# Graph layer with resnorm: the edge products of a group in one burst every second turn, its sum behind the next burst, attention earlier

## Chip, core and metric

One core of a Trainium2 chip runs the whole program. The time is device microseconds of one execution; the kernel before took 1297.51 us (median of three runs, 1295.53 to 1299.25). Five engines work from queues of their own, each in its own order, and meet at semaphores only: TensorE (PE; PEld is its weight loading), VectorE (DVE), ScalarE (ACT), GpSimd (POOL) and SyncE (SP, which issues DMAs).

## What is computed

There are 8192 nodes with 256 values each and 131072 edges, sorted by destination, with 64 values each. All of it is float32.

```python
msg = relu(x[src] + edge_attr @ w_e + b_e)
agg = segment_sum(msg, dst)
h_local = bn1(relu((x + agg) @ w1 + b1) @ w2 + b2 + x)
h_attn = bn2(attention(x in blocks of 32 nodes, 4 heads) @ out_w + out_b + x)
out = h_local + h_attn
out = bn3(out + relu(out @ m_w1 + m_b1) @ m_w2 + m_b2)
result = layernorm(x + out)
```

## The kernel before

**Edges.** They are worked through in 128 groups of 1024, each of four pairs (a pair q is two tiles of 128 edges, 128x512 numbers), in 256 turns of two pairs; eight more turns end the program. For a pair, POOL gathers the rows of x by two indirect DMAs into one of seven buffers `xg` (L430); before every second pair it waits until the pair six earlier has been read (L427). For 14 of the 512 pairs SP and ACT fetch the rows instead, one DMA a row (L329, L463). DVE adds b_e to the rows and puts the sum into one of four PSUM banks (`seed`, L681: "additions of b_e"); the bank must have been read by the message four pairs earlier. PE adds the edge product on top (`products(d)`, L867: eight matmuls for the two pairs of turn d). ACT makes the message by relu into SBUF (`message`, L469). 

**Sums.** PE sums a group's four messages with a one-hot matrix (`sum_group`, L882, 16 matmuls, "S"), ACT copies the sum (`copy_agg`, L474, "C"), PE transposes the copy (`transpose_agg`, L891, two transposes, "X"), and DVE adds it to `aggT` at the places of the group's destinations (`add_agg`, L714, four additions, "A"). S of the next group waits for A of this one, since both use bank G. In the kernel before, S of group n ends turn 2n+1 on PE, C ends the same turn on ACT, and X comes in turn 2n+2 behind the products of that turn.

**Attention** goes over 16 slabs J of 512 nodes. Its steps have fixed turns, counted from `heads_base(J)`: q, k (each in two halves, ACT adds the bias as it copies: L482, L490), scores (PE, L938), maximum and subtraction on DVE (L726, L731), exponential on ACT (L496), normalising and transposing on DVE (L738 to L747), v, and the product with v ("av"), both copied by ACT. **Node blocks** b (12 of 512 nodes, 6 of 256, 4 of 128) have plans of the same kind, `NODES`, `NODES_256` with `FIRST_256`, and `NODES_128`: w1 (PE; ACT makes h1, L515), B (PE adds attention's output product and w2's; DVE makes `o`, L758; ACT makes z, L523), m1 (ACT makes h2, L529), m2 (DVE adds, L767), T (PE transposes; DVE adds x and takes the statistics, L779 to L787), log and y (ACT, DVE), out. All PE products of attention and blocks have line 837, that of the helper `product`.

**Order.** Each engine has a loop over turns, and in a turn a fixed order. PE: products, X, attention, node steps, S. ACT: messages, copies of attention, of node steps, C, then its row DMAs. DVE: additions of b_e for the next turn, A, one-hot matrix, attention, node steps. An engine that comes to a wait stands until it is met, and all that is behind it in its queue stands too. SP issues the loads and stores in the order of turns.

Of the kernel before, what the change touches and what calls it, by code (L numbers as in the profile page):

```python
# [15 lines left out]
CC = C // 128  # L16
P = 128
TG = 8
GE = TG * P
NG = E // GE  # L20
PG = TG // 2
NP = NG * PG
# [37 lines left out]
def heads_base(J):  # L60
    return max(16 * J - 12, 12 * J)

# [7 lines left out]
             "y": (7,), "xn": (2,), "out": (8,)}  # L70
FIRST_256 = {12: 211, 13: 217, 14: 223, 15: 229, 16: 235, 17: 243}
NODES_128 = {
# [8 lines left out]
}  # L81
LASTB = 21


SUMS = {2 * n + 1: n for n in range(NG)}
TURNS = 264
# [27 lines left out]
def before(b, stage):  # L114
    return sum(uses(n, stage) for n in range(b))
# [9 lines left out]
def nodes_in(turn, stages):  # L125
    found = []
    for b in range(len(BLOCKS)):
        if b < 12:
            plan, base = NODES, 16 * b + 19
        elif b < 18:  # L130
            plan, base = NODES_256, FIRST_256[b]
        else:
            plan, base = NODES_128[b], 0
        found += [(b, s, n) for s in stages for n, at in enumerate(plan[s]) if base + at == turn]
    return found
# [89 lines left out]
def program(nc, k):  # L225
# [3 lines left out]
    with ExitStack() as ctx:  # L229
# [47 lines left out]
        def cols(b):  # L277

            w = BLOCKS[b][1]
            at = 0 if w == FULL else b % 2 * 256  # L280
            return slice(at, at + w)
# [36 lines left out]
        def _(sp):  # L318
# [44 lines left out]
            for turn in range(TURNS):  # L363
# [5 lines left out]
                if turn in (2, 12):  # L369
                    load_xT(1 if turn == 2 else 2)  # L370
                if turn % 16 == 13 and NXT <= (turn + 19) // 16 < NJ:
                    load_xT((turn + 19) // 16)
                for J, _, pair in heads_in(turn - 1, ("av",)):
# [66 lines left out]
        def _(act):  # L440
# [101 lines left out]
            for turn in range(TURNS):  # L542
                for q in (2 * turn, 2 * turn + 1):
                    if q < NP:
                        message(q)
                for J, stage, n in heads_in(turn, ("q", "k", "soft", "v", "av")):
                    attention(J, stage, n)
                for b, stage, use in nodes_in(turn, ("z", "w1", "m1", "log")):
                    node(b, stage, use)
                if turn in SUMS:  # L550
                    copy_agg(SUMS[turn])
                for row in range(ACT_ROWS * ROWS):
                    if act_turn(row) == turn:
                        fetch_row(SP_ROWS + row // ROWS, row % ROWS)
# [5 lines left out]
        def _(dve):  # L560
# [245 lines left out]

            seed(0)
            seed(1)
            make_onehot(0)
            for turn in range(TURNS):  # L810
                for q in (2 * turn + 2, 2 * turn + 3):
                    if q < NP:
                        seed(q)
# [20 lines left out]
        def _(pe):  # L834
# [135 lines left out]
            def node(b, stage, use):  # L970
                n0, w = BLOCKS[b]
                at, to = cols(b), bank(b, stage)
                J, of_slab = part(b)
                if stage == "w1":
# [13 lines left out]
                    for c, of in chunks(b, "w1", use):  # L988
                        ins = product(to[:, of], CC, lambda a: k.w1[:, a, c * P:(c + 1) * P],
                                      lambda a: aggT[:, a, n0:n0 + w])  # L990
                    ins.then_inc(s_p1, 1)
                if stage == "B":
                    early = b == LASTB
                    if use:
                        pe.wait_ge(s_o, before(b, "B") + use)
                    else:
                        pe.wait_ge(s_oc, (n0 + w + NB - 1) // NB)
                    if early:
                        for c, of in chunks(b, "B", use):
                            product(to[:, of], CC, lambda a: k.owT[:, a, c * P:(c + 1) * P],  # L1000
                                    lambda a: k.oT[:, J % NOT, a, of_slab], start=c == 0,
                                    stop=False, skip=True)
                    if not use:
                        pe.wait_ge(s_h1, before(b + 1, "w1"))
# [36 lines left out]

            for turn in range(TURNS):
                if turn < ND:
                    products(turn)
                if turn - 1 in SUMS:
                    transpose_agg(SUMS[turn - 1])
                weights(turn)
                for J, stage, n in heads_in(turn, ("q", "k", "sc", "v", "av")):
                    attention(J, stage, n)
                for b, stage, use in nodes_in(turn, ("T", "m2", "m1", "B", "w1")):  # L1050
                    node(b, stage, use)
                if turn in SUMS:
                    sum_group(SUMS[turn])
            with pe.If(pe.value_load(k.bad_i[0:1, 0:1], min_val=0, max_val=1) > 0):
                pe.wait_ge(s_go, 1)
                general_tensor(nc, k, g, pe)
# [309 lines left out]
```

## Time and profile before

| | |
|---|---|
| median of three runs | 1297.51 us |
| the profiled execution, time of its own | 1296.03 us |
| its span, from first to last instruction | 1294.2 us |
| PE busy | 1154.5 us (89%) |
| POOL busy | 944.9 us (73%) |
| DVE, ACT busy | 826.7 us (64%), 541.2 us (42%) |
| granted TensorE clock, mean | 0.969 |

Busy time of an engine is the union of its instructions. The time around them is either a wait for something that the profile names, or "issue": the engine waited for nothing that the profile shows. POOL's 73% are the instructions that write the gathers' descriptors; between two of them there is a fixed stretch of "issue". ACT's row DMAs count as issue too, not as busy.

### The profile page before, as it was taken

To read this page: it belongs to the slowest core of one execution; us is meant where nothing else is said; L and a number is where in the kernel's file an instruction comes from. 1 tells how busy PE (TensorE), PEld (TensorE's weight loads), DVE (VectorE), ACT (ScalarE), POOL (GpSimd) and SP (SyncE) were. 2 spreads that over 40 slices of the span, in tenths; PEclk is the share of its full clock that TensorE was granted. 3 is DMA by queue.
4 is the path that set the end of the run, shared out by engine and by line. 5 is a ranking of instruction groups with operands and counts; after the bars stand their busy time and mean duration, and the time that the engine had idled before them with its cause. 6 is when DMAs were issued, how large, how long until landed. Compare 5 with 4: busy or idle time off the path is not lost.

```text
span 1294.2 us, 28246 instructions
## 1 busy us (share of the span) xinstructions
PE 1154.5 (89%) x7309; PEld 647.4 (50%) x7309; DVE 826.7 (64%) x2090; ACT 541.2 (42%) x1077; POOL 944.9 (73%) x1004
## 2 busy tenths in 40 slices
PE   6787989998899899998989999998989998998896
PEld 3444454544445444444544545454444555765675
DVE  5847486767566576755758666575756667557563
ACT  1343434444344435434344443443434443443353
POOL 7777777777777777777777777777777777675770
PEclk7898999999999999999999999999999998999999
DMA  8554555655555555565555555555655565554550
GB/s 316 154 170 141 175 156 175 174 173 180 170 165 169 164 182 172 160 183 148 183 173 175 165 165 176 166 175 174 172 164 154 183 183 147 168 160 126 175 155 26
DMA packets 119282, 216.50 MB, mean 167 GB/s; under 512 B 24784, under 2 KB 69584, under 8 KB 119120
## 3 DMA queue, kind: packets, MB, share of 16 engines
q0 software_dynamic: 47808, 130.61, 35.0%
q1 hardware_dynamic: 67312, 79.47, 19.6%
q10 hardware_dynamic: 4000, 4.61, 1.0%
q8 instruction: 59, 0.97, 0.3%
q14 instruction: 103, 0.84, 0.2%
HBM read 197.82 MB, written 16.78 MB: 166 GB/s over the span
## 4 chain that ended last, share of the span: by engine, by line
PE 58%; DVE 11%; ACTq 8%; ACT 7%; issue 7%; POOL 6%; DMA 2%; DVEq 0%; SPq 0%
PE bank L837 33%; PE bank L867 12%; PE bank L882 7%; POOL xg L430 6%; ACTq L463 6%; ACT msg L469 4%; DVE bank L681 3%; PE bank L891 3%; ACTq L311 2%; DVE dif L731 2%; DVE mx L726 2%; PE bank L938 1%; DMA xT<-in_xT_dram 1%; DVE aggT L714 1%; ACT kbd L490 1%
## 5 line engine op out<-in xcount | busy, mean ns | idle before, releaser
L430 POOL DMA_INDIRECT xg<-in_x_dram,srcs x996 | 944.0, 948 | 317.4 <-issue 290.0
L469 ACT ACTIVATE msg<-bank 128x512 f32<-128x512 f32 x512 | 277.8, 595 | 543.6 <-PE bank L867 286.7
L681 DVE TENSOR_TENSOR bank<-xg,bank 128x512 f32<-128x512 f32 x498 | 327.4, 690 | 138.1 <-DMA xg<-in_x_dram,srcs 93.0
L867 PE MATMUL bank<-we,ea 64*128 64x256 f32 x2048 | 301.7, 415 | 35.5 <-DVE bank L681 35.5
L867 PEld LDWEIGHTS bank<-we,ea 64*128 64x128 f32 x2048 | 183.1, 192 | 179.7 <-issue 124.1
L714 DVE TENSOR_TENSOR aggT<-bank,aggT 128x64 f32 x512 | 115.2, 225 | 169.1 <-PE bank L891 115.2
L882 PE MATMUL bank<-msg,onehot 128*32 128x256 f32 x2048 | 141.1, 394 | 49.0 <-ACT msg L469 48.4
L837 PE MATMUL bank<-xT,iwT 128*128 128x512 f32 x256 | 128.2, 624 | 7.6 <-DMA xT<-in_xT_dram 4.0
L837 PE MATMUL bank<-o,m 128*128 128x512 f32 (+2 forms) x352 | 125.6, 491 | 4.6 <-DVE o L758 4.4
L882 PEld LDWEIGHTS bank<-msg,onehot 128*32 128x32 f32 x2048 | 54.4, 111 | 141.6 <-ACT msg L469 96.9
L837 PE MATMUL bank<-h,m 128*128 128x512 f32 (+2 forms) x352 | 116.6, 479 | 2.1 <-ACT h L529 2.1
L837 PEld LDWEIGHTS bank<-o,m 128*128 128x128 f32 x352 | 60.7, 193 | 41.3 <-issue 27.9
L837 PEld LDWEIGHTS bank<-h,m 128*128 128x128 f32 x352 | 60.0, 190 | 41.3 <-issue 34.9
L837 PE MATMUL bank<-aggT,w 128*128 128x512 f32 (+2 forms) x176 | 66.1, 510 | 15.7 <-DVE xn L779 13.8
L474 ACT COPY agg<-bank 128x256 f32<-128x256 f32 x128 | 47.5, 371 | 70.8 <-PE bank L882 67.2
L837 PEld LDWEIGHTS bank<-xT,iwT 128*128 128x128 f32 x256 | 45.4, 198 | 51.9 <-issue 46.0
L767 DVE TENSOR_TENSOR z<-bank,z 128x512 f32<-128x512 f32 (+2 forms) x44 | 23.1, 543 | 72.1 <-PE bank L837 71.9
L891 PE MATMUL bank<-ident,agg 128*128 128x128 f32 x256 | 57.7, 308 | 7.5 <-ACT agg L474 7.5
L837 PE MATMUL bank<-iwT,xT 128*128 128x256 f32 x256 | 64.3, 395 | 0.0
L837 PE MATMUL bank<-oT,owT 128*128 128x512 f32 (+2 forms) x176 | 63.6, 485 | 0.0
L529 ACT ACTIVATE h<-bank,mb 128x512 f32<-128x512 f32 (+2 forms) x88 | 47.5, 570 | 37.3 <-PE bank L837 36.9
L837 PE MATMUL bank<-h,w 128*128 128x512 f32 (+2 forms) x176 | 62.1, 476 | 0.0
(92 smaller groups left out, 938.9 us busy)
## 6 DMA issues: line engine op xcount, KB each, us to landing
rows<-in_x_dram SPq DMA_DIRECT2D x2304, 1.0 KB
ea<-in_ea_dram SPq DMA_DIRECT2D x128, 256.0 KB
rows<-in_x_dram ACTq DMA_DIRECT2D x1280, 1.0 KB
xg<-in_x_dram,srcs POOLq DMA_INDIRECT x996
xT<-in_xT_dram SPq DMA_DIRECT2D x32, 256.0 KB, 4.2
aggT<-in_xT_dram SPq DMA_DIRECT2D x32, 256.0 KB, 4.0
oT_dram<-oT SPq DMA_DIRECT2D x32, 256.0 KB
xn<-in_x_dram SPq DMA_DIRECT2D x32, 256.0 KB
```

The costliest lines, as they stand in the source:

```text
L311: _, of = nc.values_load_multi_w_load_instructions(k.of_rows[at:at + 1, col:col + LOADED], engines=(engine,), min_val=0, max_val=(N - 1) * ...
L430: pool.indirect_dma_start(xg[:, slot % NX, n * C:(n + 1) * C], None, t["x"], bass.IndirectOffsetOnAxis(k.srcs[:, at:at + 1], 0)).then_inc( ...
L463: act.dma_start(row_bytes[e:e + 1, row_buffer(n), two * 4 * C:(two + 1) * 4 * C], x_bytes[0:1, bass.ds(of_row[0][i % LOADED], 4 * C)]).the ...
L469: nc.scalar.activation(msg[:, q % NM, :], EA[q % 4][:, :], ACT.Relu).then_inc(s_msg, 1)
L474: nc.scalar.copy(k.agg[:, :], G[:, 0:C]).then_inc(s_agg, 1)
L529: ins = nc.scalar.activation(k.h2[:, c, at], bank(b, "m1")[:, of], ACT.Relu, bias=k.mb1[:, c:c + 1])
L681: nc.vector.tensor_tensor(EA[q % 4][:, :].rearrange("p (a c) -> p a c", a=2), pair.rearrange("p (a c) -> p a c", a=2), KB[:, 0:C].unsqueez ...
L714: nc.vector.tensor_tensor(window, sums[:, :, sub * W:(sub + 1) * W], window, ALU.add).then_inc(s_added if sub == SUB - 1 else s_part, 1)
L837: ins = nc.tensor.matmul(to, stationary(c), moving(c), start=start and c == 0, stop=stop and c == blocks - 1, skip_group_check=skip)
L867: ins = nc.tensor.matmul(EA[(2 * d + pair) % 4][:, two * C:(two + 1) * C], ea[rows, n % NEA, at:at + P], k.we[rows, :], start=False, stop= ...
L882: ins = nc.tensor.matmul(G[sub * W:(sub + 1) * W, 0:C], onehot[:, n % 2, at, :], msg[:, q % NM, two * C:(two + 1) * C], start=tile == 0, s ...
L891: ins = nc.tensor.transpose(G[:, c * P:(c + 1) * P], k.agg[:, c * P:(c + 1) * P], ident[:, :])
```

## The change

PE makes the products of two turns, a whole group, at the start of every even turn. ACT's four messages and DVE's four additions of b_e for the next group follow at even turns. S of group n moves from the end of turn 2n+1 to turn 2n+2, right behind the burst of group n+1, and X to the start of turn 2n+3, where no products stand before it; the last 14 groups keep S at turn 2n+1. ACT's C stays the last copy of the turn in which S is, and in ACT's queue it is still behind that turn's copies for attention and blocks. From slab 6 on attention begins five turns earlier than before (slabs 4 and 5: two and four), the blocks of 512 one turn later, those of 256 one turn later but for the last. SP loads the slabs of xT three turns earlier. From turn 254 on PE's order is written out by hand.

```diff
 def heads_base(J):
-    return max(16 * J - 12, 12 * J)
+    return max(16 * J - 17, 12 * J if J < 3 else 14 * J - 6)
-FIRST_256 = {12: 211, 13: 217, 14: 223, 15: 229, 16: 235, 17: 243}
+FIRST_256 = {12: 212, 13: 218, 14: 224, 15: 230, 16: 236, 17: 243}
...
-SUMS = {2 * n + 1: n for n in range(NG)}
+CLOSE = NG - 14
+SUMS = {(2 * n + 2 if n < CLOSE else 2 * n + 1): n for n in range(NG)}
...
-            plan, base = NODES, 16 * b + 19
+            plan, base = NODES, 16 * b + 20
...
-                if turn % 16 == 13 and NXT <= (turn + 19) // 16 < NJ:
-                    load_xT((turn + 19) // 16)
+                if turn % 16 == 10 and NXT <= (turn + 22) // 16 < NJ:
+                    load_xT((turn + 22) // 16)
...
-                for q in (2 * turn, 2 * turn + 1):
-                    if q < NP:
+                if turn % 2 == 0 and turn < ND:
+                    for q in range(2 * turn, 2 * turn + PG):
                         message(q)
...
-                for q in (2 * turn + 2, 2 * turn + 3):
-                    if q < NP:
+                if turn % 2 == 0 and 2 * turn + PG < NP:
+                    for q in range(2 * turn + PG, 2 * turn + 2 * PG):
                         seed(q)
...
-            for turn in range(TURNS):
-                if turn < ND:
+            for turn in range(LAST_TURN):
+                if turn % 2 == 0:
                     products(turn)
+                    products(turn + 1)
+                if SUMS.get(turn, NG) < CLOSE:
+                    sum_group(SUMS[turn])
                 if turn - 1 in SUMS:
                     transpose_agg(SUMS[turn - 1])
                 weights(turn)
...
-                if turn in SUMS:
+                if SUMS.get(turn, 0) >= CLOSE:
                     sum_group(SUMS[turn])
+            transpose_agg(NG - 2)
+            products(ND - 2)
+            products(ND - 1)
+            node(19, "T", 0)
+            node(20, "w1", 0)
+            sum_group(NG - 1)
+            node(20, "A", 0)
+            transpose_agg(NG - 1)
+            node(20, "B", 0)
+            node(LASTB, "A", 0)
+            node(LASTB, "w1", 0)
+            node(20, "m1", 0)
+            node(LASTB, "B", 0)
+            node(LASTB, "m1", 0)
+            node(20, "m2", 0)
+            node(LASTB, "m2", 0)
+            node(20, "T", 0)
+            node(LASTB, "T", 0)
```

The stage "A" is attention's half of B, done ahead of h1.

## Rows read from the trace of the kernel before

**Rows 1.** Stretches: us, busy time of each engine (instructions), PE clock, DMA, GB/s.
```profile
120.00:1050.00 930.00, 853.61 (x5241) 442.96 (x5238) 604.12 (x1506) 398.89 (x773) 703.07 (x743) 0.98 0.57 170
1050.00:1294.20 244.20, 215.98 (x1514) 153.28 (x1512) 143.26 (x391) 102.74 (x232) 152.70 (x162) 0.97 0.47 140
...
1120.00:1160.00 40.00, 39.30 (x246) 26.09 (x246) 21.07 (x57) 18.86 (x39) 27.34 (x29) 1.00 0.57 171
```
**Rows 2.** The edge products alone in such a stretch: PE busy (count), PEld, clock, DMA, GB/s.
```profile
120.00:1050.00 930.00, 224.88 (x1544) 136.43 (x1540) 0.98 0.57 170
```
**Rows 3.** POOL's waits: who waited for whom, us in total, times, longest; 0:1085, then 1085:1205.
```profile
POOL xg L430 <- DVE bank L681: 10.8, 32, 0.7
...
POOL xg L430 <- DVE bank L681: 14.1, 10, 3.9
```
**Rows 4.** PE's waits from 120 to 1050.
```profile
PE bank L882 <- ACT msg L469: 40.1, 45, 2.7
PE bank L867 <- DVE bank L681: 20.9, 23, 2.8
PE bank L891 <- ACT agg L474: 7.0, 11, 0.6
PE bank L837 <- DVE xn L779: 6.7, 10, 0.8
```
**Rows 5.** Timeline of turn 199 and the next (start, us, engine, what, [idle before <-releaser]).
```profile
911.90 1.98 PE L837 MATMUL bank<-xT,iwT 128*128 128x512 f32 x4
...
913.81 1.07 PE L882 MATMUL bank<-msg,onehot 128*32 128x256 f32 x16
913.92 1.38 ACT L490 ACTIVATE kbd<-bank,vecT 64x512 f32<-64x512 f32 x2 [0.82 <-PE bank L837]
...
914.81 1.13 PE L867 MATMUL bank<-we,ea 64*128 64x256 f32 x8
...
915.32 0.81 ACT L523 ACTIVATE z<-o,c,s 128x512 f32<-128x512 f32 x1
...
916.16 0.37 ACT L474 COPY agg<-bank 128x256 f32<-128x256 f32 x1
...
916.59 0.44 PE L891 MATMUL bank<-ident,agg 128*128 128x128 f32 x2 [0.64 <-ACT agg L474]
```
**Rows 6.** Groups by line and form: busy us, mean ns of one, idle before.
```profile
L529 ACT ACTIVATE h<-bank,mb 128x512 f32<-128x512 f32 x48 | 32.9, 686 | 29.4 <-PE bank L837 29.3
```
**Rows 7.** Timeline of DVE alone, turns 200 to 203.
```profile
918.37 1.71 DVE L726 TENSOR_REDUCE mx<-bank 32x8 f32<-32x256 f32 x4
920.12 1.72 DVE L731 TENSOR_TENSOR dif<-bank,mx 32x256 f32<-32x256 f32 x4
...
924.21 0.42 DVE L738 TENSOR_REDUCE sm<-dif 128x8 f32<-128x256 f32 x1
...
925.36 1.79 DVE L747 STREAM_TRANSPOSE probT<-dif 32x256 f32<-32x256 f32 x4
927.17 1.29 DVE L681 TENSOR_TENSOR bank<-xg,bank 128x512 f32<-128x512 f32 x2
928.50 1.30 DVE L714 TENSOR_TENSOR aggT<-bank,aggT 128x64 f32 x4
```
**Rows 8.** Timeline of a block's last steps: the addition of x.
```profile
655.66 0.68 DVE L779 TENSOR_TENSOR xn<-bank,xn 128x512 f32<-128x512 f32 x1
```
**Rows 9.** The same timeline: the end of PE's longest idle time there.
```profile
660.82 1.11 PE L882 MATMUL bank<-msg,onehot 128*32 128x256 f32 x16 [2.45 <-ACT msg L469]
```
**Rows 10.** Two short stretches behind it, columns as in rows 1.
```profile
661.80:664.30 2.50, 2.50 (x14) 1.62 (x11) 0.77 (x2) 0.69 (x2) 1.89 (x3) 0.50 0.71 212
664.30:668.30 4.00, 4.00 (x12) 1.56 (x10) 3.38 (x12) 1.46 (x3) 3.08 (x4) 0.90 0.53 121
```
**Rows 11.** Timeline of the end: the last additions of b_e and the last products.
```profile
1265.31 1.28 DVE L681 TENSOR_TENSOR bank<-xg,bank 128x512 f32<-128x512 f32 x2
...
1269.93 1.13 PE L867 MATMUL bank<-we,ea 64*128 64x256 f32 x8
```

More of the change, by code:

```diff
@@ L75 @@
     19: {"w1": (250,), "B": (251,), "z": (252,), "m1": (252,), "m2": (253,), "T": (254,),
[5 rows of a table removed]
[5 rows of a table added]
 }
+LAST_TURN = 254
 LASTB = 21
-SUMS = {2 * n + 1: n for n in range(NG)}
+CLOSE = NG - 14
+SUMS = {(2 * n + 2 if n < CLOSE else 2 * n + 1): n for n in range(NG)}
 TURNS = 264
@@ L805, in node @@
                     ins.then_inc(s_y, 1)
-            seed(0)
-            seed(1)
+            for q in range(PG):
+                seed(q)
             make_onehot(0)
             for turn in range(TURNS):
-                for q in (2 * turn + 2, 2 * turn + 3):
-                    if q < NP:
+                if turn % 2 == 0 and 2 * turn + PG < NP:
+                    for q in range(2 * turn + PG, 2 * turn + 2 * PG):
                         seed(q)
@@ L971, in node @@
                 n0, w = BLOCKS[b]
-                at, to = cols(b), bank(b, stage)
+                at, to = cols(b), bank(b, "B" if stage == "A" else stage)
                 J, of_slab = part(b)
@@ L991, in node @@
                     ins.then_inc(s_p1, 1)
+                if stage == "A":
+                    pe.wait_ge(s_oc, 2 * NJ)
+                    if b < LASTB:
+                        pe.wait_ge(s_h1, before(b + 1, "w1"))
+                    for c, of in chunks(b, "B", use):
+                        product(bank(b, "B")[:, of], CC,
+                                lambda a: k.owT[:, a, c * P:(c + 1) * P],
+                                lambda a: k.oT[:, J % NOT, a, of_slab], start=c == 0,
+                                stop=False, skip=True)
                 if stage == "B":
-                    early = b == LASTB
+                    early = b >= 20
                     if use:
@@ L997, in node @@
                         pe.wait_ge(s_oc, (n0 + w + NB - 1) // NB)
[L998 to L1003, printed above, removed]
                         pe.wait_ge(s_h1, before(b + 1, "w1"))
```

10 rows, old and new, of the table NODES_128 are left out of this document.

## Prediction

> **What bounds the kernel now.** I read the stretches first, for one calm part of the run, 120 to 1050 us. There were 1544 edge products, eight a turn, so 193 turns in 930 us: 4.82 us a turn, 77.1 us for 16 turns, the period of a node block [rows 1, 2]. Two engines could set that. POOL wrote 743 gathers in it, 1.25 us each without a break [rows 1]; its waits for a free buffer are 10.8 us in the first 1085 us, while 1085 to 1205 has 14.1 [rows 3]. So POOL sets the pace up to 1085, and only there behind it does it stand for others. PE was busy for 853.61 of the 930 us, which is 70.8 us of every 16 turns [rows 1]; the other 6.3 are waits, and the view of waits names them: 40.1 us for messages before the sums, 20.9 for additions of b_e before the products, 7.0 for the copy of the sum, 6.7 for a block's last addition [rows 4]. These waits are the shape that PE's spare time takes while gathers set the pace: 6.3 us in 16 turns, 0.8 in two. To take one away moves the spare time elsewhere and gains nothing; to add more than 0.8 us to every two turns makes PE the pace-setter. The change is judged by that number.
>
> **The burst.** It is the same matmuls in another order: two times 1.13 us [rows 5]; cost 0. Four messages follow in about 2.4 us (a 512-wide copy on ACT takes 0.69 [rows 6]), and four additions at 0.65 each [rows 7], each behind its message, so the next group's banks are ready some 4.5 us after a burst began. Between two bursts PE has 70.8/8 less 2.2, or 6.6 us of other work [rows 1, 5]: hidden. Without that cover it would be 2 us a group.
>
> **The gathers.** A buffer is freed by an addition; four now come in a row, once in two turns. POOL may run six pairs ahead, and a group takes it 10 us: a first addition may come some 12 us behind the landing of the group before without a stop. Taken at 0 where POOL would set the pace. If DVE is later (behind 2.9 of normalising and 3.5 of maximum and subtraction [rows 7]) by 1 to 2 us once in 16 turns, it costs 12 to 24 us in all; I keep that for a rival. The 14 pairs fetched row by row are wanted one to three turns earlier, of six or nine turns that the plan gives them: 0.
>
> **Sums behind the burst.** The wait for messages goes: 40.1 us in the calm part, 3.3 of the 6.3 us [rows 4]. With POOL as the pace it is worth nothing by itself.
>
> **The copy of the sum.** Here a new wait arises. Before, a product of the keys ended at 913.88, ACT then made its two copies (1.38 us), z (0.81) and the copy of the sum (0.37), and the transposes began at 916.59, 2.7 us behind the product [rows 5]. Of these PE had covered 2.1 with the sum and the next turn's products (1.07 and 1.13); 0.64 was left as idle time. After the change the burst and the sum stand ahead of the even turn's attention and block steps, the transposes directly behind them, and ACT's copy of the sum is still the last of its turn. PE then stands through whatever ACT has to copy for the last step of the even turn, plus the copy, with nothing to cover it; behind the transposes stand all steps of the odd turn and the next burst. The eight even turns of a period, say 192 to 206, with 0.1 us for two handovers: after q 0.69+0.37+0.1 = 1.2 [rows 5, 6]. After k 1.38+0.37+0.1, of which a block's four transposes hide about 0.6 (two took 0.44): 1.2. After w1 1.2. At turn 198 there is no product behind the sum, and ACT's copy stands behind the exponential of the second scores, which waits for DVE. DVE does four additions, the normalising, A, and maximum and subtraction in a row, 2.6+2.9+1.3+3.5 = 10.3 us [rows 7], plus statistics and y that I leave out for the lower bound; PE reaches the same point after two w1 products, a copy wait, the scores, burst and sum, about 9.9. Two copies follow, so the wait is 1.3 at least, 3.6 with statistics and y: I take 3.0. After v and after av ACT has z as well: 0.69+0.81+0.37+0.1 = 2.0 each. After m1, twice, 1.2 each. Sum: 1.2+1.2+1.2+3.0+2.0+2.0+1.2+1.2 = 13.0.
>
> **VectorE's order.** A stands behind four additions instead of two; the sum of the next group waits for A (1.3 [rows 7]) and is now early in the turn: 0 to 0.7 in most turns, taken as 0.6 in all. The block's last addition (0.68 [rows 8]) now stands behind maximum and subtraction (3.5) in turn 195, and the next w1 waits for it: 0.6 before (6.7 us in 12 periods [rows 4]), now 0.6 to 1.2, taken 0.9. ACT's row DMAs come behind the copy and before the next turn's work: 0, or 1 a period where they meet the messages.
>
> **Sum for a period.** 13.0+0.6+0.9 = 14.5; the modelled end of a PE instruction lies about 0.1 behind the start of the next [rows 5], so 0.8 comes off: 13.7. PE's own 70.8 stay. 84.5 us for 16 turns instead of 77.1: +7.4. If the copies waited only for the shortest case (turn 198 1.2, z early) 9 us would remain, 79.8: +2.7. With 18 it is 88.8: +11.7. For the early slabs (to about turn 80, 3.6 periods) scores fall on even turns, where ACT copies nothing for them: 1.5 less. Over the 193 turns, 12.06 periods: 12.06 x 7.4 - 3.6 x 1.5 = +84; bounds +33 and +141.
>
> **The end.** From 1050 on PE is busy for 215.98 of 244.2 us [rows 1]. Five turns of attention leave it, four products of 1.98 and some scores, about 9 us [rows 5]; the blocks come a turn later, one w1 product of 1.98 enters; POOL's 14.1 us of stops [rows 3] no longer matter, since POOL is then ahead. In the last 14 groups the transposes have the burst before them again, a cover of 2.2. I take -8, between 0 and -14. The tail: additions end 1266.59, last products start 1269.93, the end is 24.3 later [rows 11]. By hand the new order has the same links (sum, copy, transposes, A, w1, B, m1, m2, T of block 21); attention's halves done early fill idle time. But A of group 125 now stands behind the last four additions and the sum of 126 and the last burst behind it, some 2 us more if gathers are late, which with PE as the pace they aren't. 0, from -3 to +3. xT loads issued three turns earlier, of which each waits for a block's B, hold SP's later loads by less than a turn; edge features are loaded two groups ahead: 0.
>
> **Total.** 1296.0 (the profiled execution's own time; its span is 1294.2) + 84 - 8 = 1372. The median of the runs lies 1.5 above the profiled one, which is lost in the bounds; I leave 1372.
>
> **Rival 1, POOL stays the pace (faster).** If the new waits fit into 6.3 us a period, PE never becomes the limit, and the end gives back POOL's stops: 1296 - 14.1 = 1282. It decides at 0.8 us in two turns. For it: PE's waits are spare time now. Against it: 2.7 us from product to transposes is a row, and 2.1 of cover leaves. The Trainium skill (Perfetto Trace Analysis, Identifying the Most-Contended Engine) says that matmul busy share is no good measure for headroom, and to go by weight-load share, 443 of 930 here; with so much room this rival would win. The trace speaks against that use: from 1120 to 1160 PE is busy 39.30 of 40 us while POOL falls to 27.34 [rows 1], so full PE does hold up the gathers.
>
> **Rival 2, bursts stop the gathers.** The copy is hidden in most turns, but POOL stops 1 to 2 us a period for buffers: +24 at most, so 1318.
>
> **Rival 3, a lower clock.** After PE's longest wait of a period, 2.45 us [rows 9], the granted clock is 0.50 for 2.5 us and 0.90 for the next 4 [rows 10], that is 1.2 of 2.4 GHz at first; the time lost is 2.5 x 0.5 + 4 x 0.1 = 1.6 us. Now that happens once in a period. With two more such waits in a period: 12 x 2 x 1.6 = 38, 1410. The skill (TensorE: Matmul & The Clock Gate, "HAM oscillation — how this bites in real kernels") has the same: idle time between bursts of matmuls returns them to half the clock again and again, which speaks against gathering products into bursts. The mean clock of the calm part is 0.98 [rows 1], so far a small matter.
>
> **Chances.** Forecast 0.66 (own range 1330 to 1405), rival 3 0.12, rival 2 0.07, rival 1 0.15. Range 1318 to 1425: it takes in rivals 2 and 3 and the bounds of the copy wait, and leaves out rival 1 and little more. About 0.3% is what a measurement of this kernel can tell from no change. Faster 0.13, same 0.04 (rival 1 half realised), slower 0.83.
>
> **What would show it.** Right: PE's waits put down to ACT's copy of the sum at L891 rise from 7.0 to over 100 us in the middle, those for messages at L882 vanish, POOL waits for additions through the whole run, turns take about 5.3 us each. Wrong: POOL's gathers still without a break up to 1085, or the copy of the sum ending before PE is through with the even turn's steps.

## The result, and the profile after

The changed kernel takes 1419.51 us (median of four runs, 1416.42 to 1422.43), the kernel before 1297.89 us beside it: a ratio of 1.0939, 95% interval 1.091 to 1.0967. It is slower by 121.6 us. The profiled execution took 1422.43 us, its span is 1420.7 us, its mean granted clock 0.946.

Lines of the changed kernel are numbered a little higher: products L869, additions of b_e L683, messages L471, sums L884, their copy L476, transposes L893, A L716, the helper L839, the gathers L432. First the stretches, columns as in [rows 1]; the last line is the edge products alone, as in [rows 2].

```profile
120.00:1150.00 1030.00, 858.92 (x5239) 462.42 (x5238) 601.97 (x1504) 391.24 (x772) 708.40 (x750) 0.96 0.52 154
1120.00:1160.00 40.00, 33.74 (x205) 17.78 (x203) 20.68 (x52) 15.82 (x32) 28.42 (x31) 1.00 0.54 159
1240.00:1420.70 180.70, 143.56 (x1040) 108.31 (x1032) 92.19 (x262) 66.09 (x160) 90.91 (x96) 0.93 0.39 116
...
120.00:1150.00 1030.00, 192.01 (x1536) 140.44 (x1536) 0.96 0.52 154
```

1536 products are 192 turns, in 1030 us: 85.8 us for 16 turns, where [rows 1, 2] gave 77.1. In sum PE's matmuls hardly grew, 858.92/12 = 71.6 us against 70.8 (two shifts cancel in it: see rival 3 below). What grew is its waiting, 6.3 to 14.2 us. The view of PE's waits for the same stretch (who waited for whom, total, times, longest) says for what, to be laid beside [rows 4]:

```profile
PE bank L893 <- ACT agg L476: 142.4, 95, 3.3
PE bank L839 <- DVE xn L781: 12.6, 8, 1.9
PE bank L884 <- DVE aggT L716: 12.5, 12, 3.2
PE bank L940 <- DVE dif L733: 2.9, 1, 2.9
PE bank L869 <- DVE bank L683: 0.5, 1, 0.5
```

The wait for messages ahead of the sums (40.1 us) is gone, that for additions of b_e (20.9) nearly so, and the transposes now wait for the copy of the sum in 95 of the 96 groups, 1.5 us each. The gathers answer to [rows 3]: POOL's waits for a free buffer in 120 to 1150 us.

```profile
POOL xg L432 <- DVE bank L683: 112.5, 64, 7.7
```

It stands for buffers throughout, where [rows 3] had it nearly without a break. One period of PE's timeline, turns 194 to 208, shows the wait turn by turn (start, us, what, idle before and its releaser; the other instructions are left out):

```profile
896.63 0.44 PE L893 MATMUL bank<-ident,agg 128*128 128x128 f32 x2 [1.43 <-ACT agg L476]
...
906.16 0.44 PE L893 MATMUL bank<-ident,agg 128*128 128x128 f32 x2 [1.04 <-ACT agg L476]
...
916.40 0.69 PE L893 MATMUL bank<-ident,agg 128*128 128x128 f32 x2 [3.26 <-ACT agg L476]
...
931.50 0.44 PE L893 MATMUL bank<-ident,agg 128*128 128x128 f32 x2 [1.65 <-ACT agg L476]
...
940.98 0.44 PE L893 MATMUL bank<-ident,agg 128*128 128x128 f32 x2 [1.66 <-ACT agg L476]
...
950.95 0.44 PE L893 MATMUL bank<-ident,agg 128*128 128x128 f32 x2 [1.95 <-ACT agg L476]
...
958.99 0.44 PE L893 MATMUL bank<-ident,agg 128*128 128x128 f32 x2 [1.04 <-ACT agg L476]
...
970.47 0.44 PE L893 MATMUL bank<-ident,agg 128*128 128x128 f32 x2 [1.04 <-ACT agg L476]
```

They add up to 13.1 us. The first of them in full, PE and ACT: the place that [rows 5] shows for the kernel before.

```profile
892.78 1.98 PE L839 MATMUL bank<-xT,iwT 128*128 128x512 f32 x4
894.60 0.60 PE L1043 MATMUL bank<-ident,z 128*128 128x128 f32 x4
...
894.80 0.68 ACT L492 ACTIVATE kbd<-bank,vecT 64x512 f32<-64x512 f32 x1 [1.70 <-PE bank L839]
...
895.50 0.68 ACT L492 ACTIVATE kbd<-bank,vecT 64x512 f32<-64x512 f32 x1
...
896.20 0.37 ACT L476 COPY agg<-bank 128x256 f32<-128x256 f32 x1
```

PE was through with the sum when the product began, but ACT made the two copies of the keys first, because they stand ahead of it in its queue. PE had a block's four transposes as cover, and then nothing.

To compare kernels, the span is divided at the starts of turns 20 and 212 (the 161st and the 1697th edge product); us of the profiled executions:

| kernel | to turn 20 | turns 20 to 212 | turn 212 to end | span |
|---|---|---|---|---|
| before | 119.6 | 928.0 | 246.6 | 1294.2 |
| changed | 121.7 | 1032.0 | 266.9 | 1420.7 |
| copy first | 120.2 | 964.9 | 265.0 | 1350.2 |
| end turn by turn | 121.6 | 1035.6 | 251.8 | 1409.0 |
| copy first, end turn by turn | 121.8 | 965.3 | 243.7 | 1330.8 |
| copy first, attention back | 120.4 | 956.5 | 255.7 | 1332.6 |
| these three together | 119.9 | 953.1 | 234.4 | 1307.5 |
| sums put back | 128.4 | 1023.6 | 266.4 | 1418.5 |
| sums put back, additions in odd turns | 123.4 | 992.0 | 251.2 | 1366.6 |
| before + bursts | 131.1 | 992.8 | 287.4 | 1411.3 |
| before + bursts, blocks later | 127.9 | 1033.5 | 267.8 | 1429.2 |
| before + attention earlier | 119.8 | 959.4 | 243.6 | 1322.9 |
| before + sums later | 120.6 | 939.8 | 240.4 | 1300.8 |
| before + late part | 118.5 | 937.9 | 233.9 | 1290.4 |

So 2.1 us were lost at the start, 104.0 in the middle, 20.3 at the end.

### The profile page after: what moved, and what is told of

Its sections match the earlier page's. It is cut to its first block, busy times and chain, and to the rows that moved or that the text cites. A ratio compares the mean times of both kernels' runs of the same rounds, so it can differ in the third digit from the quotient of the medians.

```text
span 1420.7 us, 28248 instructions
## 1 busy us (share of the span) xinstructions
PE 1161.7 (82%) x7309; PEld 677.6 (48%) x7309; DVE 820.8 (58%) x2090; ACT 528.8 (37%) x1077; POOL 943.8 (66%) x1004
## 4 chain that ended last, share of the span: by engine, by line
PE 53%; DVE 18%; ACTq 10%; ACT 7%; issue 7%; POOL 3%; DMA 1%; SPq 1%; DVEq 1%
PE bank L839 33%; PE bank L869 9%; ACTq L465 7%; PE bank L884 5%; ACT msg L471 3%; DVE bank L683 3%; POOL xg L432 3%; DVE mx L728 3%; DVE dif L733 3%; PE bank L893 3%; ACTq L313 2%; DVE aggT L716 2%; PE bank L966 2%; ACT agg L476 2%; DVE probT L749 2%
## 5 line engine op out<-in xcount | busy, mean ns | idle before, releaser
L432 POOL DMA_INDIRECT xg<-in_x_dram,srcs x996 | 942.9, 947 | 439.7 <-issue 277.4
L683 DVE TENSOR_TENSOR bank<-xg,bank 128x512 f32<-128x512 f32 x498 | 312.0, 691 | 244.3 <-ACT msg L471 225.4
L471 ACT ACTIVATE msg<-bank 128x512 f32<-128x512 f32 x512 | 264.8, 602 | 384.7 <-PE bank L869 304.3
L869 PE MATMUL bank<-we,ea 64*128 64x256 f32 x2048 | 265.4, 400 | 6.3 <-DVE bank L683 4.9
L869 PEld LDWEIGHTS bank<-we,ea 64*128 64x128 f32 x2048 | 193.1, 192 | 107.5 <-issue 85.8
L716 DVE TENSOR_TENSOR aggT<-bank,aggT 128x64 f32 x512 | 115.2, 225 | 184.1 <-PE bank L893 130.0
L893 PE MATMUL bank<-ident,agg 128*128 128x128 f32 x256 | 58.2, 311 | 164.7 <-ACT agg L476 164.7
L884 PE MATMUL bank<-msg,onehot 128*32 128x256 f32 x2048 | 139.2, 389 | 16.5 <-DVE aggT L716 16.4
L839 PE MATMUL bank<-o,m 128*128 128x512 f32 (+2 forms) x352 | 134.2, 519 | 15.6 <-DVE o L760 11.0
L893 PEld LDWEIGHTS bank<-ident,agg 128*128 128x128 f32 x256 | 26.7, 145 | 233.7 <-ACT agg L476 229.3
L839 PE MATMUL bank<-xT,iwT 128*128 128x512 f32 x256 | 128.3, 625 | 2.0 <-DMA xT<-in_xT_dram 1.2
L839 PE MATMUL bank<-h,m 128*128 128x512 f32 (+2 forms) x352 | 116.6, 479 | 2.3 <-ACT h L531 2.3
L884 PEld LDWEIGHTS bank<-msg,onehot 128*32 128x32 f32 x2048 | 55.0, 110 | 81.2 <-issue 33.3
L839 PEld LDWEIGHTS bank<-o,m 128*128 128x128 f32 x352 | 63.6, 208 | 55.0 <-issue 33.7
L839 PEld LDWEIGHTS bank<-h,m 128*128 128x128 f32 x352 | 61.4, 190 | 50.4 <-issue 45.2
L839 PE MATMUL bank<-aggT,w 128*128 128x512 f32 (+2 forms) x176 | 66.2, 510 | 20.0 <-DVE xn L781 14.1
L839 PE MATMUL bank<-iwT,xT 128*128 128x256 f32 x256 | 79.1, 464 | 0.0
L839 PE MATMUL bank<-oT,owT 128*128 128x512 f32 (+2 forms) x176 | 71.4, 534 | 2.4 <-ACT h L517 2.3
L839 PEld LDWEIGHTS bank<-xT,iwT 128*128 128x128 f32 x256 | 44.6, 194 | 48.0 <-issue 45.9
L492 ACT ACTIVATE kbd<-bank,vecT 64x512 f32<-64x512 f32 x64 | 43.7, 682 | 64.0 <-PE bank L839 63.6
```

Of the source, the lines that this page charges most:

```text
L432: pool.indirect_dma_start(xg[:, slot % NX, n * C:(n + 1) * C], None, t["x"], bass.IndirectOffsetOnAxis(k.srcs[:, at:at + 1], 0)).then_inc( ...
L471: nc.scalar.activation(msg[:, q % NM, :], EA[q % 4][:, :], ACT.Relu).then_inc(s_msg, 1)
L492: ins = nc.scalar.activation(k.kbd[of, n, :, h, :], X[of, :].rearrange("p (r n) -> p r n", n=GW), ACT.Identity, bias=vecT[of, V_INB + 2 + ...
L683: nc.vector.tensor_tensor(EA[q % 4][:, :].rearrange("p (a c) -> p a c", a=2), pair.rearrange("p (a c) -> p a c", a=2), KB[:, 0:C].unsqueez ...
L716: nc.vector.tensor_tensor(window, sums[:, :, sub * W:(sub + 1) * W], window, ALU.add).then_inc(s_added if sub == SUB - 1 else s_part, 1)
L839: ins = nc.tensor.matmul(to, stationary(c), moving(c), start=start and c == 0, stop=stop and c == blocks - 1, skip_group_check=skip)
```

## The experiments

**Is it the copy's place in ACT's queue?** In the changed kernel only C moves, directly behind the four messages, except for the last 14 groups.

```diff
                         message(q)
+                if SUMS.get(turn, NG) < CLOSE:
+                    copy_agg(SUMS[turn])
                 for J, stage, n in heads_in(turn, ("q", "k", "soft", "v", "av")):
...
-                if turn in SUMS:
+                if SUMS.get(turn, 0) >= CLOSE:
                     copy_agg(SUMS[turn])
```

> The changed kernel with one thing moved: up to group 113 ScalarE copies the sum directly behind the four messages, ahead of the turn's copies for attention and blocks. Theory A (TensorE stands for the copy of the sum, behind ScalarE's other copies): the waits at L893 for the copy fall from 142 us in the middle to under 20, sixteen turns take 77 to 79 us again instead of 85.8, and the time is 1419.5 - 105 = 1315 (1305 to 1330). Rival B (the bursts themselves, four messages and four additions in a row, hold up the turn): the waits move to other lines and the time stays above 1390.

Measured: 1351.1 us, ratio 1.0424 (1.0401 to 1.0447). Of the 121.6 us lost 68.4 came back, in the table nearly all of it in turns 20 to 212 (67.1 of 70.5). PE's largest waits in 120 to 1040 us (lines two higher; the first was 126.8 in this window of the changed kernel):

```profile
PE bank L895 <- ACT agg L476: 27.9, 32, 2.6
PE bank L841 <- DVE xn L783: 21.5, 8, 3.3
PE bank L886 <- DVE aggT L718: 20.8, 13, 3.3
```

The copy's place is the largest single part in this kernel, but about 36 us less than theory A expected: the waits for the block's addition and for A grew from 11.0 and 11.9 to 21.5 and 20.8.

**The end.** The bursts undone from turn 228 on, without and with the copy first (products, messages and additions of a turn in their own turn again):

```diff
+SPLIT = 228
...
-                if turn % 2 == 0:
+                if turn >= SPLIT:
+                    products(turn)
+                elif turn % 2 == 0:
                     products(turn)
                     products(turn + 1)
```

> The changed kernel, from turn 228 on again with products, messages and additions turn by turn. Theory D (in the last 28 turns, where a block's steps follow each other turn by turn, four messages and four additions stand in front of the copies and additions that the next step waits for): these turns take 156 to 162 us instead of 180.7, 1419.5 - 20 = 1395 to 1402. Rival E (they are slow for another reason: the order of sums, or the late arrival): no change, 1415 to 1425.

> Both changes of the first two experiments on the changed kernel together: copy of the sum behind the messages up to group 113, and turn by turn from turn 228 on. If the two terms are separate (the copy costs the middle, the bursts cost the end) they add: 1351 - 13 = 1338 (1333 to 1344). If the end was slow because the middle arrives late and not because of the bursts, nothing more is gained than by the copy alone: 1351.

Measured: 1407.41 (ratio 1.0852, 1.0832 to 1.0871) and 1331.89 us (1.0258, 1.0236 to 1.028). The first lies between the theories at 12 us less, the second is 19 us below the kernel with the copy first and just under its expected range. In the table the end falls by 15.1 and by 21.3 us, to about what it was before (246.6). Turns 228 to 254 by themselves took 127.7 us before, 145.6 in the changed kernel, and 128.6 and 128.0 with the bursts undone. So the bursts cost 15 to 21 us at the end, and what undoing them gives back comes on top of what the copy gives back. How they cost it, in the changed kernel's timeline of block 17 and the next (PE, then ACT, then DVE):

```profile
1309.95 1.89 PE L839 MATMUL bank<-o,m 128*128 128x256 f32 x8
1315.51 3.43 PE L839 MATMUL bank<-o,m 128*128 128x256 f32 x8 [3.67 <-ACT h L531]
...
1335.34 3.58 PE L839 MATMUL bank<-aggT,w 128*128 128x256 f32 x8 [4.30 <-DVE aggT L716]
...
1349.23 3.63 PE L839 MATMUL bank<-o,m 128*128 128x256 f32 x8 [3.54 <-DVE o L760]
...
1341.78 2.05 ACTq L465 DMA_DIRECT2D rows<-in_x_dram  x5
1343.88 0.60 ACT L471 ACTIVATE msg<-bank 128x512 f32<-128x512 f32 x1 [3.49 <-issue]
...
1344.58 2.49 DVE L683 TENSOR_TENSOR bank<-xg,bank 128x512 f32<-128x512 f32 x4 [7.78 <-ACT msg L471]
...
1348.31 0.86 DVE L760 SCALAR_TENSOR_TENSOR o<-xT,s,bank 128x256 f32<-128x256 f32 x2
```

The burst ended at 1341.80, but ACT was issuing row DMAs until 1343.83 (ACTq, the issuing in its queue). Four messages follow, DVE stands at four additions that need them (7.78 us idle), then A and `o`, for which PE waits 3.54 us. Turn by turn only two messages and two additions stand in that chain, and the additions need messages of the turn before. The products behind each of the three waits take 3.43 to 3.63 us where eight of the same shape took 1.89 at 1309.95: the clock, below.

**Attention.** Alone on the kernel before, and taken back in the kernel with the copy first (there the two lines run the other way):

```diff
-    return max(16 * J - 12, 12 * J)
+    return max(16 * J - 17, 12 * J if J < 3 else 14 * J - 6)
...
-                if turn % 16 == 13 and NXT <= (turn + 19) // 16 < NJ:
-                    load_xT((turn + 19) // 16)
+                if turn % 16 == 10 and NXT <= (turn + 22) // 16 < NJ:
+                    load_xT((turn + 22) // 16)
```

> The kernel before with the earlier attention alone (and the earlier loads of xT). Theory A: it is not what costs; gathers set the pace in the middle and the last turns get lighter by five turns of attention: 1285 to 1297. A rival C, in which the new phase of attention against the blocks (scores on odd turns, exponentials on even ones) makes the waits: the middle slows to 80 us or more for sixteen turns, 1330 or more.

> The changed kernel with the copy of the sum behind the messages, and attention in the turns that it had before. Theory P (the new places of attention cost the middle some 32 us by themselves, as they did without bursts): 1351 - 30, that is 1315 to 1328. Theory Q (with bursts the new places are the better ones: in the old ones the subtraction of the scores stands on even turns, behind four additions that wait for messages): no gain or a loss, 1350 to 1380.

Measured: 1321.68 us alone (ratio 1.0194, 1.0153 to 1.0236), 1334.16 us taken back (1.0286, 1.0269 to 1.0304), 17 us below the kernel with the copy first (8.4 of them in turns 20 to 212, 9.3 at the end). Both lie between the theories. Earlier attention gained 3.0 us at the end of the kernel before and lost 31.4 in turns 20 to 212. There PE's waits for messages were 45.6 us where 39.5 had been in the same window, for additions of b_e 30.0 where 20.4 had been, and one for the keys' copy is new:

```profile
PE bank L938 <- ACT kbd L490: 8.3, 5, 2.0
```

**The sums alone.** The kernel before with S behind the next turn's products, X a turn later, and the blocks one turn later, without bursts.

```diff
-SUMS = {2 * n + 1: n for n in range(NG)}
+CLOSE = NG - 14
+SUMS = {(2 * n + 2 if n < CLOSE else 2 * n + 1): n for n in range(NG)}
...
                     products(turn)
+                if SUMS.get(turn, NG) < CLOSE:
+                    sum_group(SUMS[turn])
```

> The kernel before with the sums alone moved behind the next turn's products (and the blocks one turn later), turn by turn otherwise, so that the transposes have one turn's products (1.13 us) ahead of them. Theory A: of some 13 us of waits for the copy in sixteen turns this cover takes eight times 1.1, so 4 to 5 remain while 3.3 of waits for messages go; the middle keeps 77 to 79 us, 1295 to 1320. If the copy of the sum were held up by something that the products don't cover, the middle would go to 82 or more and the time to 1350 and above.

Measured: 1304.0 us, ratio 1.0058 (1.004 to 1.0076). Theory A. PE's waits in 120 to 1040 us:

```profile
PE bank L868 <- DVE bank L682: 58.2, 28, 3.7
PE bank L892 <- ACT agg L475: 16.4, 17, 1.8
```

Here X has one turn's products as cover again, and the wait is 16.4 us instead of 126.8. The messages' wait (39.5) went, and that for additions grew by 38: the spare time only moved.

**The bursts alone**, on the kernel before, and once more with the blocks one turn later (16 * b + 20).

```diff
-                if turn < ND:
+                if turn % 2 == 0 and turn < ND:
                     products(turn)
+                    products(turn + 1)
...
-                for q in (2 * turn, 2 * turn + 1):
-                    if q < NP:
+                if turn % 2 == 0 and turn < ND:
+                    for q in range(2 * turn, 2 * turn + PG):
                         message(q)
...
-                for q in (2 * turn + 2, 2 * turn + 3):
-                    if q < NP:
+                if turn % 2 == 0 and 2 * turn + PG < NP:
+                    for q in range(2 * turn + PG, 2 * turn + 2 * PG):
                         seed(q)
```

> The kernel before with the bursts alone: products, messages and additions of b_e of a group in one row every second turn; sums, transposes, attention and blocks stay in their turns. Theory A: the transposes keep a cover (the burst, 2.1 us), so the middle keeps its 77 us for sixteen turns; only the last 28 turns lose, as they do in the changed kernel (180.7 instead of 156.2), so 1297.5 + 10 to 25 = 1308 to 1322. Rival B: the bursts carry most of the 121 us, 1390 or more.

> The bursts alone, as in the run of bursts alone (1415 us, where TensorE waited 54 us in turns 20 to 212 for w1's slab addition on VectorE, of 65 us that this stretch had gained), with the blocks one turn later, as the change has them. Theory F: with four additions of b_e in a row on even turns, the last step of a block's old plan falls behind additions that wait for messages, and one turn more takes that wait away: 40 to 60 us less, 1355 to 1375 us. Theory G: the additions that wait for messages stand in front of everything on VectorE, and another wait takes the place of w1's: 1395 us or more.

Measured: 1415.16 us (ratio 1.0928, 1.0897 to 1.0958) and 1429.44 us (1.1007, 1.0974 to 1.104). Theories A and F missed, rival B and theory G held: alone the bursts cost about as much as the whole change, and a later turn for the blocks gives back 19.6 us at the end and costs 40.7 in turns 20 to 212. The waits in 120 to 1040 us, first of the bursts alone, then with the blocks later:

```profile
PE bank L837 <- DVE xn L779: 54.3, 11, 7.1
...
DVE bank L681 <- ACT msg L469: 305.0, 77, 7.8
```

```profile
PE bank L1038 <- DVE xn L779: 48.1, 10, 6.6
...
DVE bank L681 <- ACT msg L469: 264.6, 72, 8.0
```

DVE stands for about a third of this window at additions whose banks the messages haven't read yet (30.3 us in the kernel before, 128.6 in the changed one). The block's last addition stays late wherever its turn is (w1 waits for it in the first, the next transposes in the second); why one turn more left that wait standing isn't settled.

**The sums put back in the changed kernel.** S is at the end of turn 2n+1 again, so X has a whole burst as cover; bursts, attention and the blocks' turn stay as changed.

```diff
-CLOSE = NG - 14
+CLOSE = -1
...
-                if SUMS.get(turn, NG) < CLOSE:
+                if False:
                     sum_group(SUMS[turn])
...
-                if SUMS.get(turn, 0) >= CLOSE:
+                if turn in SUMS:
                     sum_group(SUMS[turn])
```

> The changed kernel with only the sums put back to the end of turn 2n+1, so that the transposes stand behind a burst again; bursts, attention's places and the blocks' later turn stay. If the copy that the transposes wait for is the largest part of the loss, as the run with the copy first (1351 us) says, this kernel has the cover back and costs 1330 to 1355 us. If the burst with its rows of messages and additions is the loss by itself, 1390 us or more.

Measured: 1422.35 us, ratio 1.098 (1.0938 to 1.1022): no gain. The cover works, X's wait falls from 126.8 to 3.8 us; others take its place (PE, DVE, ACT in 120 to 1040 us):

```profile
PE bank L884 <- DVE aggT L716: 37.3, 17, 4.4
PE bank L839 <- DVE dif L733: 29.2, 7, 4.6
...
PE bank L893 <- ACT agg L476: 3.8, 4, 1.6
...
DVE bank L683 <- ACT msg L471: 264.3, 69, 7.8
```

```profile
ACT msg L471 <- issue: 121.7, 39, 3.9
```

This is the run that keeps the story from being "the copy". A now falls in the even turn, behind four additions that wait for this turn's own messages. The messages in turn stand behind row DMAs that ACT issues after C; but the kernel before has more of that idle time (188.0 us in 75 places; the changed kernel 51.1), so it doesn't explain the loss by itself.

**Is DVE's row of additions the cause there?** The same kernel, the four additions moved to the odd turn, when their banks have long been read.

```diff
-                if turn % 2 == 0 and 2 * turn + PG < NP:
-                    for q in range(2 * turn + PG, 2 * turn + 2 * PG):
+                if turn % 2 == 1 and 2 * turn + 2 < NP:
+                    for q in range(2 * turn + 2, 2 * turn + 2 + PG):
                         seed(q)
```

> The run with the sums put back (1422 us, as slow as the change) with one more edit: VectorE's four additions of b_e for the next burst move from the even turn, in which the messages are made whose banks they need, to the odd turn behind it. Theory H: with four banks and bursts, VectorE stands in the even turn until this turn's own burst has been read (264 us in 120 to 1040 us), and the group's addition A, the attention's and the blocks' steps that stand behind it come late for TensorE; moved, that wait falls below 100 us, TensorE's waits for VectorE (aggT 37, dif 35 us) mostly go, and the time is 1340 to 1380 us. Theory K: the additions then come too late for the burst and free the gather buffers later, TensorE waits for the additions and GpSimd longer than its 103 us: 1410 us or more.

Measured: 1366.75 us, ratio 1.054 (1.0511 to 1.0569), 55.6 us less, theory H. The waits for messages on DVE, and the new one of PE for the additions:

```profile
DVE bank L683 <- ACT msg L471: 14.1, 20, 1.3
```

```profile
PE bank L869 <- DVE bank L683: 29.3, 20, 3.6
```

PE's wait for A, 37.3 us, is no longer in the list, that for `dif` fell from 35.5 to 13.8. A piece of theory K came true beside it, the 29.3 us; the other didn't, POOL's waits fell from 102.9 to 71.6. The rest of this kernel's loss is spread over copies of ACT (kbd, qT, h: 55 us together).

**What is left.** Three parts undone: copy first, attention's old places, the end turn by turn.

> The changed kernel with three parts undone: the copy of the sum directly behind the messages, attention and xT loads at the old places, the end from turn 228 turn by turn. Additive: 1334 less the 19 us that the end took from the run with the copy first gives 1315 us (1312 to 1322), of which some 10 us above the kernel before are left in turns 20 to 212 and the rest in the end. If attention's old places had already given back the same part of the end (255.7 against 265.0 us there), 1324 to 1332 us.

Measured: 1309.25 us, ratio 1.0093 (1.0065 to 1.0121), 6 us under the additive 1315 and under its range: 110 of the 121.6 us are back. The end is now shorter than before the change (234.4 against 246.6), the middle still 25.1 longer; 19.2 of these fall in turns 20 to 84 (329.1 us against 309.9), and why isn't settled.

**A version faster than both.** The kernel before in its middle, with PE's order of the end by hand and the plans of blocks 19 to 21 from the change, and only slabs 13 to 15 of attention (and their xT loads) three to five turns earlier.

```diff
-    return max(16 * J - 12, 12 * J)
+    return max(16 * J - 12, 12 * J) if J < 13 else 16 * J - 17 + (15 - J)
...
-            for turn in range(TURNS):
+            for turn in range(LAST_TURN):
```

> The kernel before with two parts of the change alone, where gathers do not set the pace: the hand-written order from turn 254 on, and attention of the last three slabs three to five turns earlier. The middle is untouched, 77 us for sixteen turns. From turn 254 to the end 24 to 25 us instead of 28.4, and up to 3 us from the lighter last turns: 1288 to 1294. If the last turns are set by the chain of sums and not by TensorE's load, 1294 to 1299.

Measured: 1292.11 us, ratio 0.996 (0.9944 to 0.9976): 5.2 us faster than the kernel before. From turn 254 on the span is 25.0 us instead of 28.4; up to there the profiled executions take 1265.4 and 1265.8. So, by the table, what gains is PE's order by hand with the plans of blocks 19 to 21, the one part of the change that was found to gain; moving the last slabs of attention brought nothing that shows.

## Why the prediction was right, and where it was off

**The direction, the place and rather more than half of the size were right**: +76 us forecast, +121.6 measured. The pace passed from POOL to PE, the wait that did most of it is the one named, and all four signs named beforehand came (a turn takes 5.36 us). But 1419.5 lies above the forecast's own range (1330 to 1405) and 5.5 us inside the outer one, which had been drawn to take in a lower clock: that the range held is partly luck.

**The copy of the sum** was forecast at 13.0 us of idle time a period; the period shown has 13.1, the mean of twelve is 142.4/12 = 11.9. Single terms miss by up to 0.75 us (1.95 instead of 1.2 behind the first m1) and cancel. The dearest place was named too. Turn 198, PE, ACT and DVE:

```profile
912.07 1.07 PE L884 MATMUL bank<-msg,onehot 128*32 128x256 f32 x16 [0.60 <-DVE aggT L716]
916.40 0.69 PE L893 MATMUL bank<-ident,agg 128*128 128x128 f32 x2 [3.26 <-ACT agg L476]
916.88 3.62 PE L839 MATMUL bank<-iwT,xT 128*128 128x256 f32 x8
920.29 2.98 PE L839 MATMUL bank<-oT,owT 128*128 128x512 f32 x4
...
915.67 0.42 ACT L498 ACTIVATE dif<-dif 128x256 f32<-128x256 f32 x1 [2.03 <-DVE dif L733]
...
915.99 0.35 ACT L476 COPY agg<-bank 128x256 f32<-128x256 f32 x1
...
913.91 1.72 DVE L733 TENSOR_TENSOR dif<-bank,mx 32x256 f32<-32x256 f32 x4
```

C waits behind the exponential, which waits for DVE's subtraction, which stands behind the four additions and A: 3.26 us, forecast 3.0. A was forecast at 0.6 a period, w1's wait for T at 0.9; they came to 1.04 and 1.05. The sum for a period, 84.5, measured 85.8.

**The early periods were mis-sized**: forecast 1.5 us cheaper each up to turn 80. Periods two to four took 84.8 to 85.5 us like all others, and the first, turns 20 to 36, took 96.7 (79.9 before), with 17.6 us of stops of POOL in 121 to 219 us and a clock of 0.93 there. The eleven periods behind it average 85.0 us, +7.9 each where 7.4 was forecast, together +87; with the first one's +16.8 that makes the 104.0 us of the middle where +84 stood. What makes the first so dear isn't settled.

**The end was the step that failed.** Forecast -8, measured +20.3 us from turn 212 on: +6.9 in turns 212 to 228, +17.9 up to 254, and -4.4 from there on (24.0 us instead of 28.4, where the tail had been taken at 0). Its working looked at what left the stretch (attention) and at PE's spare time, not at the chain of a 256 block, in which each step waits for ACT or DVE, and in which four messages and four additions in a row now stand. Nor was the gain hidden behind the bursts: with them undone turns 228 to 254 take 128.6 and 128.0 us, no less than the 127.7 before, although attention is still the earlier one, and with the copy first, taking attention back shortened the end by 9.3 us. So no run shows the 9 us taken for attention's leaving; alone, on the kernel before, earlier attention gave 3.0 at the end. Start +2.1, middle +104.0, end +20.3 on 1296.0 give 1422.4, the profiled time.

**"The burst: cost 0" holds only beside the other parts.** The prediction priced the burst by its matmuls and by whether the banks are ready for the next one (they were: PE's wait for additions is 0.5 us). It put each addition behind its message, but it didn't price that DVE, with four banks for four additions, stands there until this turn's messages have read them, and all that is behind them in its queue with it. Alone the bursts cost some 120 us. In the changed kernel the moved sum brings A, X and all that follows them into the odd turn, clear of those additions, and opens the copy's wait instead. Either way 1415 to 1430 us. That separation is the reason is argued from the two kernels in which A or the additions stand in odd turns (1351 and 1367 us); the second shows it for the additions directly. The standing as such needn't cost much: with three parts undone DVE still stands 124.1 us in 120 to 1040, at 1309 us. So no single part "is" the loss: of the changed kernel 68 us go with the copy's place, then about 17 with attention and 25 with the end.

**Attention earlier was priced in the middle only through the copy's wait** (turn 198, the early slabs), and costs 25 us alone, with no bursts and the copy covered. It sets scores on odd and the exponential on even turns; that this makes the waits is argued, as no run moved the phase by itself.

**The rivals.** Rival 1 (POOL stays the pace, 1282) fell with POOL's 112.5 us of waits. The Trainium skill's rule named there (Perfetto Trace Analysis, Identifying the Most-Contended Engine) would have found even more room after the change, weight loads being 462 of 1030 us; no such room showed: waits of 14.2 us in 16 turns, where 6.3 had been, went into the time. A sentence of the same page (Optimization Strategy), that a gap repeating for a stretch on the engine that should be saturated can mean too little SBUF or PSUM for the next tile, fits in part: with the sums put back the gaps for want of a bank are DVE's, 264.3 us, and reach PE through what stands behind them. Rival 2 (stops of POOL, 24 us at most, with the copy hidden) fell too: the copy is not hidden, and POOL's stops follow a PE that is late: with only the copy moved they fall from 102.6 to 40.6 us in 120 to 1040. Rival 3, a lower clock, is there, mean 0.969 to 0.946, but as part of the loss, not in place of the forecast.

Its size doesn't show in PE's busy time, which grew by only 0.8 us a period, because the burst itself got cheaper. The edge products took 224.88 us for 193 turns and take 192.01 for 192, 18.6 and 16.0 us a period (part of it can be the modelled end, which a burst has once instead of twice); all else went from 52.1 to 55.6. Of these 3.5 some 2 are the two kinds of products that follow the wait of turn 198: from 120:1050 before to 120:1150 after, in the mean, `iwT,xT` went from 390 to 466 ns and `oT,owT` from 605 to 693, 24 us in twelve periods.

## What to carry to other kernels

Before work is moved on one engine, write down for each wait what is queued ahead of its releaser on the other engine and what still covers that; here 2.1 us of cover for a 2.7 us path left, and 0.8 us in two turns was all there was to lose. A burst needs buffers for more than itself: where a burst fills all of them, the engine that refills them stands until the burst has been read, and everything in its queue stands too, so put the refill where the buffers are already free (56 us here), or behind what others wait for. Price an edit in the stage with the longest chain (the tail) separately from the steady state, and test parts in more than one combination: one part undone showed 68 us, its counterpart undone nothing.

## What the runs showed of the hardware

**The clock.** Granted clock of the stretches behind the waits of 3.26 (two lines), 4.30 and 3.54 us (columns as in [rows 1]):

```profile
916.90:921.00 4.10, 4.10 (x10) 3.02 (x10) 3.96 (x9) 0.46 (x1) 2.40 (x3) 0.50 0.34 108
921.00:925.00 4.00, 4.00 (x10) 1.51 (x8) 2.54 (x8) 0.13 (x1) 3.09 (x4) 0.81 0.62 184
...
1335.30:1339.00 3.70, 3.66 (x12) 2.48 (x16) 1.39 (x6) 0.04 (x1) 2.79 (x4) 0.54 0.53 151
...
1349.20:1352.80 3.60, 3.57 (x10) 2.53 (x10) 0.31 (x1) 1.09 (x2) 2.84 (x3) 0.53 0.38 112
```

That is 1.2 of 2.4 GHz for most of each, and eight products that took 1.89 us take 3.4 to 3.6, so such a wait costs some 1.7 us more than itself. Behind the first, the next four took 2.98 at a clock of 0.81 (1.98 at 892.78), one more. This agrees with [rows 9, 10], and with the Trainium skill (TensorE: Matmul & The Clock Gate, "HAM oscillation — how this bites in real kernels"), which has idle time between bursts of matmuls send them back to half the clock.

**ACT's row DMAs hold up what is behind them.** They don't count as busy, but the messages at 1343.88 came after 3.49 us of idle time in which ACT issued them. The sum of such idle time is no price, though: before messages, in 120 to 1040 us, it is 188.0 us in the kernel before, 121.7 with the sums put back and 51.1 in the changed kernel. What it costs depends on who waits for the messages, and no run moved the row DMAs, so their share in the loss is open.
